# Down-projection of a routed expert layer: wide products on TensorE, the halves summed on VectorE, row weights picked on ScalarE

## What is computed

```
xn  = layernorm(x)
out = x + attn(xn) + ffn(xn)
attn: k = xn @ W_z.T + b_z ; gates by softplus ; cumulative sum over the 256 channels,
      running log-sum-exp over the 1024 steps, one mean and deviation over everything,
      exp, + xn, layernorm with ln_w, ln_b
ffn:  router_logits = xn @ w_gate.T ; softmax ; top 2 of 8 experts, weights made to sum to 1
      for e in 8: h = silu(xn @ w1[e].T) * (xn @ w3[e].T)        # 704 wide
                  out += h @ w2[e].T * expert_weight
```

## Time and profile before

| | us |
|---|---|
| median of the runs shown (356.61 to 356.78) | 356.72 |
| the profiled execution: its own time | 357.79 |
| the profiled execution: its span, first to last instruction | 356.1 |

### The profile page before, as it was taken

How to read it: one execution, slowest core, us unless ns; L and a number is a source line. 1 busy time by engine, 2 the same in 40 slices (tenths; PEclk the granted TensorE clock), 3 DMA queues, 4 the chain that set the end, 5 groups by cost and what they waited for, 6 DMA issues and landing times.

```text
span 356.1 us, 6682 instructions
## 1 busy us (share of the span) xinstructions
PE 325.8 (91%) x1964; PEld 273.9 (77%) x1964; DVE 260.8 (73%) x466; ACT 219.9 (62%) x328; POOL 206.4 (58%) x137
## 2 busy tenths in 40 slices
PE   8998999799999999999898999999999999979830
PEld 8883464588878898997787899889898988969730
DVE  5488787989996899889899842584589668763300
ACT  2547997455879974999854269934853485323400
POOL 4500023159968674989899728563885475945331
PEclk9999969989999999999999999999999999999985
DMA  7924912005444542354354434542463534354621
GB/s 263 426 120 137 293 52 59 15 11 150 122 82 115 142 101 32 80 129 129 44 144 109 102 38 115 142 101 33 84 181 89 75 45 76 47 76 49 98 38 15
DMA packets 19086, 37.00 MB, mean 104 GB/s; under 512 B 2272, under 2 KB 13536, under 8 KB 19008
## 3 DMA queue, kind: packets, MB, share of 16 engines
q0 software_dynamic: 9168, 11.97, 21.5%
q1 hardware_dynamic: 8496, 22.56, 20.4%
q10 hardware_dynamic: 1376, 1.85, 1.4%
HBM read 27.45 MB, written 11.03 MB: 108 GB/s over the span
## 4 chain that ended last, share of the span: by engine, by line
PE 54%; DVE 23%; ACT 8%; issue 8%; DMA 2%; ACTq 1%; POOL 1%; POOLq 0%; DVEq 0%
PE PS L1296 23%; PE PS L1314 11%; PE PS L1190 6%; PE PS L1326 5%; DVE wrow L1067 3%; DVE tmp L961 3%; PE PS L1176 2%; DMA out<-work,sidx 2%; DVE hT L956 2%; DVE U L985 2%; DVE A L998 1%; PE PS L1220 1%; DVE xrow L1054 1%; DVE xrow L1059 1%; PE PS L1265 1%
## 5 line engine op out<-in xcount | busy, mean ns | idle before, releaser
L1296 PE MATMUL PS<-wbuf,xT 128*128 128x512 f32 (+1 forms) x648 | 149.6, 384 | 4.9 <-issue 3.7
L1296 PEld LDWEIGHTS PS<-wbuf,xT 128*128 128x128 f32 x648 | 118.3, 190 | 29.4 <-issue 9.3
L424 POOL TENSOR_TENSOR wbuf<-raw,wbuf x28 | 81.4, 2924 | 23.1 <-ACT wbuf L604 21.4
L406 POOL DMA_INDIRECT out<-work,sidx x35 | 62.7, 1792 | 53.2 <-ACT work L621 20.1
L1314 PE MATMUL PS<-wbuf,hT 128*128 128x256 f32 x648 | 86.8, 288 | 0.0
L1314 PEld LDWEIGHTS PS<-wbuf,hT 128*128 128x128 f32 x648 | 79.3, 189 | 1.9 <-issue 1.9
L390 POOL DMA_INDIRECT work<-xn_dram,gidx x39 | 50.4, 1292 | 51.8 <-DVE gidx L892 36.1
L595 ACT ACTIVATE tmp<-PS 128x512 f32<-128x512 f32 x72 | 32.0, 460 | 41.6 <-PE PS L1296 41.3
L961 DVE TENSOR_TENSOR tmp<-tmp,PS 128x512 f32<-128x512 f32 x72 | 35.0, 516 | 29.4 <-ACT tmp L595 28.6
L956 DVE TENSOR_TENSOR hT<-PS,hT 128x768 fp32r<-128x768 f32 x36 | 34.2, 949 | 29.3 <-ACT hT L590 24.2
L621 ACT ACTIVATE work<-PS,wrow 128x256 f32<-128x256 f32 x35 | 16.4, 470 | 38.0 <-PE PS L1314 38.0
(11 more groups left out here) (185 smaller groups left out, 350.7 us busy)
## 6 DMA issues: line engine op xcount, KB each, us to landing
raw<-w_main SPq DMA_DIRECT2D x24, 544.0 KB
raw<-w_main SPq DMA_DIRECT2D x8, 416.0 KB
xn_dram<-xrow SPq DMA_DIRECT2D x4, 516.0 KB, 7.2
out<-xrow POOLq DMA_DIRECT2D x4, 512.0 KB, 6.1
xrow<-x SPq DMA_DIRECT2D x4, 256.0 KB, 4.8
xrow<-x ACTq DMA_DIRECT2D x4, 256.0 KB, 5.4
small_sb<-small ACTq DMA_DIRECT2D x1, 768.0 KB, 7.9
work<-xn_dram,gidx POOLq DMA_INDIRECT x39
```

Source lines behind the costliest of these rows:

```text
L406: pool.indirect_dma_start(out, bass.IndirectOffsetOnAxis(sidx[:, j:j + 1], 0), ysb[:, j % DEEP, :], None, compute_op=ALU.add).then_inc(s_s ...
L424: pool.tensor_tensor(lo, raw[:, ds(part, WP)], hi.bitcast(fp32), ALU.subtract).then_inc(s_w, 1)
L1296: ins = pe.matmul(PS[:, at:at + cols], xT[:, slot, xpart, q * P:(q + 1) * P], wbuf[:, w, wpart, q * 2 * F + at:q * 2 * F + at + cols], sta ...
```

## The change

Four things change together.

- `down(j)`: the six pieces of the high part of h are each multiplied once by both parts of the weights, side by side (512 columns into a whole PSUM bank, `y_both`), where there were two products of 256 columns. The low part of h is then multiplied by the high part of the weights, into the first half. The result is the sum of the two halves.
- `y_copy(j)` on ScalarE takes only the first half. A new `y_add(j)` on VectorE adds the second half times the row weight; the scatter-add now waits for that (`s_y`), and `y_add` for the copy (`s_ya`). `down(j)` waits for `y_add(j - 1)`.
- The row weight is picked by ScalarE (`row_weight`), ahead of any table load, and no longer by VectorE (`slot_weight`). So that one multiply-add does it, the first extra column of `xrow` becomes the difference of the two routing weights, which is one small VectorE instruction more in the routing part.
- The last tile's y is summed in `last_add`, on VectorE.

```diff
-        y_ps = PS[:, 6 * 512:6 * 512 + D]
+        y_ps = [PS[:, 6 * 512 + n * D:6 * 512 + (n + 1) * D] for n in range(2)]
+        y_both = PS[:, 6 * 512:7 * 512].rearrange("p (n d) -> p n d", n=2)
...
+            def row_weight(j):
+
+                k = j % DEEP
+                act.wait_ge(s_gt[k], 16 * (j // DEEP + 1))
+                act.activation(wrow[:, j:j + 1], xg[:, k, D:D + 1], ACT.Identity, scale=first_pick[:, j:j + 1],
+                               bias=xg[:, k, D + 1:D + 2]).then_inc(s_ws, 1)
...
-                act.activation(ysb[:, j % DEEP, :], y_ps, ACT.Copy, scale=wrow[:, j:j + 1]).then_inc(s_y, 1)
+                act.activation(ysb[:, j % DEEP, :], y_ps[0], ACT.Copy, scale=wrow[:, j:j + 1]).then_inc(s_ya, 1)
...
                     x_hi(j + 1, u % 2)
+                    row_weight(j + 1)
                 if table:
                     act.preload_act_table_set(table)
...
-            dve.tensor_tensor(xrow[:, :, D + 1], w12[:, 1, :], xrow[:, :, D], ALU.mult).then_inc(s_rw, 1)
+            step(dve.tensor_tensor(xrow[:, :, D + 1], w12[:, 1, :], xrow[:, :, D], ALU.mult))
+            dve.tensor_tensor(xrow[:, :, D], xrow[:, :, D], xrow[:, :, D + 1], ALU.subtract).then_inc(s_rw, 1)
...
+            def y_add(j):
+
+                dve.wait_ge(s_ya, j + 1)
+                dve.scalar_tensor_tensor(ysb[:, j % DEEP, :], y_ps[1], wrow[:, j:j + 1], ysb[:, j % DEEP, :],
+                                         ALU.mult, ALU.add).then_inc(s_y, 1)
...
                     x_lo(j + 1, u % 2)
-                    slot_weight(j + 1)
                 if hooks:
                     between(j)
+                y_add(j - 1)
                 h_lo(j)
...
+                    for c in range(HC):
+                        pe.matmul(y_both, hT[:, 0, c * P:(c + 1) * P], wbuf[:, w, :, W13 + c * D:W13 + (c + 1) * D],
+                                  start=(c == 0), stop=False)
+                    hold(pe, s_hlo, j + 1)
+                    for c in range(HC):
+                        ins = pe.matmul(y_ps[0], hT[:, 1, c * P:(c + 1) * P],
+                                        wbuf[:, w, 0, W13 + c * D:W13 + (c + 1) * D],
+                                        start=False, stop=(c == HC - 1))
```

More of the change, by code:

```diff
@@ L259, in build_program @@
         s_dn = sem("down_done")
-        s_y = sem("y_copied")
+        s_ya = sem("y_high_copied")
+        s_y = sem("y_summed")
         s_st = sem("rows_added")
@@ L583, in _ @@
             x_hi(1, 1, xT1_ps)
+            act.wait_ge(s_idx, 1)
+            row_weight(0)
+            row_weight(1)
             h_part(3)
@@ L724, in last_copy @@
                 hold(act, s_dn, used)
-                act.activation(hst[:, 0:D], y_ps, ACT.Copy, scale=wrow[:, NCOL:NCOL + 1]).then_inc(s_y, 1)
+                act.activation(hst[:, 0:D], y_ps[0], ACT.Copy, scale=wrow[:, NCOL:NCOL + 1]).then_inc(s_ya, 1)
             tail(act, tile, last_copy)
@@ L1061, in last_norm @@
                 ins.then_inc(s_p2, 1)
[L1063 to L1068, removed]
             softplus(0)
@@ L1076, in _ @@
             x_lo(0, 0, xT0_ps)
-            slot_weight(0)
             softplus(2)
@@ L1080, in _ @@
             x_lo(1, 1, xT1_ps)
-            slot_weight(1)
             dve.wait_ge(s_u0b, 2)
@@ L1166, in _, with last_add @@
                     tile(i, u, True)
-            tail(dve, tile)
+            def last_add(used):
+                hold(dve, s_ya, used)
+                dve.scalar_tensor_tensor(hst[:, 0:D], y_ps[1], wrow[:, NCOL:NCOL + 1], hst[:, 0:D],
+                                         ALU.mult, ALU.add).then_inc(s_y, 1)
+            tail(dve, tile, last_add)
         @block.tensor
```

## The result

The changed kernel takes 359.42 us (median; 358.22 to 360.75) where the kernel before takes 356.96 (355.92 to 358.39) beside it: a ratio of 1.0068, 95% interval 1.0053 to 1.0082, or +2.4 us (+1.9 to +2.9). The profiled execution took 358.49 us with a span of 356.7; before they were 357.79 and 356.1. The difference of these two is smaller than that of the medians because tile 0 began 1.2 us earlier in the execution after (TensorE's granted clock was 0.979 of full speed there over the span and 0.969 in the one before; the difference lies in the start: 0.97 against 0.94 up to 60 us, 1.00 against 0.91 from 60 to 80 us, and 1.00 in both from 80 to 340 us). So I compare traces from the end of tile 1's gate on.

What follows compares the result with a forecast made beforehand. Bound by TensorE, VectorE or ScalarE depending on the tile, then by GpSimd's queue from tile 26 on. Terms -0.25 + 1.9 + 0.8 + 0 + 0.45 = +2.9 us on 356.72 gave 359.6 us, range 357.0 to 362.0.

Steps and rivals of the forecast that it cites:

- Down-projection: TensorE's products: time goes with columns, so merging saves 0.02 us a tile, -0.25 us over about 12 tiles.
- L1067 leaving VectorE: VectorE: the next two-input instruction takes over the wait for GpSimd's split, or other engines pace the tile; 0 us.
- `row_weight` on ScalarE: One-column ACTIVATE of 0.20 us, counting in tiles 10, 11, 19 and 20, which ScalarE paces; +0.8 us.
- `y_add` on VectorE: 0.38 us each in tiles 2, 3, 15, 16 and 13 or 14, without waiting at the port; +1.9 us.
- Tile 11: A 3.76 us wait ahead of `h_lo` goes, but ScalarE and the tile 12 scan take the gain back; 0.
- y's owner: Scatter-add of tile 25 waits for `y_add`, ready 0.45 us behind ScalarE's copy; +0.45 us, bound 2.2.
- the case of 361.4 us: At tile 25 VectorE is still in `row_stats`, so y is ready at 272.4: +2.2 us.
- The rest of the queue rigid: Behind tile 25's scatter-add, about 85 us of GpSimd issues, landings and splits shift unchanged to the end.
- the order at the port: Rival: VectorE's scans get ahead of GpSimd's L424, each giving back up to 2.9 us; 353.8 us, chance 0.10.
- TensorE by instructions: Rival: a product costs the same at any width, saving 8.5 us over 12 tiles; 351.3 us, chance 0.02.
- no change: Rival: VectorE's additions fit in gaps, or tile 12's scan wins and ScalarE's 0.20 is hidden; 356.7 to 357.4, chance 0.12.
- slower by more: Rival: `y_add` waits for GpSimd's split because of its SBUF scalar, up to 2.5 us each; 363.9 us, chance 0.08.

Runs made afterwards that it cites:

- e2: The kernel before with only the row weight moved from VectorE to ScalarE; 357.43 us, 0.9995 of before.
- e4: The changed kernel without the sum on VectorE, second half of y left out, scatter-adds waiting for ScalarE's copy again; 357.42 us, 1.0006 of before.
- e1: The changed kernel with the row weight back on VectorE; 359.47 us, 1.0055 of before.
- e7: The changed kernel with a second VectorE sum of the same shape ahead of each `y_add`, into an unread buffer; 361.36 us, 1.0117 of before.
- e3: The changed kernel with the sum moved ahead of `row_stats` in tiles 20 to 27; 360.51 us, 1.0094 of before.
- e5: The changed kernel with the sum left out for the rows of tiles 17 on; 359.97 us, 1.007 of before.
- e8: The changed kernel with `y_add` cut to one column, all waits kept; 359.16 us, 1.0063 of before.
- e11: The changed kernel with the 18 narrow products and no sum for rows of tiles 0 to 16; 358.55 us, 1.0056 of before.
- e12: The changed kernel without any sum, the scatter-add of tile 8 also made to wait for `h_lo` of tile 9; 356.69 us, 1.0001 of before.
- e6: The changed kernel with the sum left out for the rows of tiles 0 to 16; 357.5 us, 1.0022 of before.

## Why the prediction was right, point by point

The forecast of +2.9 us was met with +2.4, inside the range and of the sign. Its terms fared less evenly, and that they added up so well is in part luck.

*Down-projection, -0.25.* Right as far as it can be read: about -0.23 in TensorE's starts between e2 and e4, and 2.35 us a group against 2.40. The time goes with columns. Six wide products are a group of 1.65 us. The Trainium skill's TensorE: Matmul & The Clock Gate, section Back-to-back issue gap, gives 131 ns for 512 columns, 0.8 us for six by my estimate; the trace disagrees and decides.

*L1067 leaving VectorE, 0.* In tiles with two-input instructions behind it the wait passed on as forecast (`less_n`, 4.05 us). The step still failed: I forgot its own length, 0.20 us and 0.13 from its begin to the next where nothing waits. Against before, e2 is 0.07 to 0.14 us shorter in each of tiles 2, 3 and 4 and 0.2 in 9 and 10; tile 13 is 0.89 shorter, and 14 gives 0.41 of that back.

*`row_weight` on ScalarE, +0.8.* The instruction is 0.39 us long and moves the next by 0.27, where I took 0.20. In the four places that I named e2 is longer than before by 0.18, 0.14, 0.26 and 0.27 us (the times of tiles 11, 12, 20 and 21), 0.85 in all, so that the term is right; but tiles 6, 7 and 8 pay 0.26, 0.19 and 0.26 too, which I had missed. With what the term above gives back, the balance from tile 1 to 28 is zero, and e1 and e2 measured about that. Their sum in the forecast was +0.8.

*`y_add` on VectorE, +1.9.* The size agrees with the trace of the kernel after, 0.98 + 0.94 us over e4 in tiles 1 to 10 where I had five times 0.38, and e7 nearly doubles it. The places are right in part: I gave tiles 2, 3, 13 or 14, 15 and 16 one each (their times are those of tiles 3, 4, 14 or 15, 16 and 17). The first two and that of tile 15 are there, 0.41 to 0.48 us each over e4, but 0.94 us arise in tiles 8 and 9, which I had called TensorE's alone. VectorE's rows in tile 9 of the kernel after show a chain with no gap, hook, sum, `h_lo`, and three more to the next gate:

```profile
139.52 2.34 DVE L988 TENSOR_TENSOR_SCAN xnT_M<-U,u 128x1024 f32<-128x1024 f32 x1
141.78 0.45 DVE L975 SCALAR_TENSOR_TENSOR work<-PS,wrow,work 128x256 f32<-128x256 f32 x1
142.15 0.94 DVE L970 TENSOR_TENSOR hT<-PS,hT 128x768 fp32r<-128x768 f32 x1
```

The others vanish among waits for splits. That it doesn't wait at the port was right (486 ns at most), with a scalar in SBUF beside one SBUF tensor: here the trace agrees with the Trainium skill's SBUF — State Buffer, section Who interferes with whom, by which at most one SBUF input does not contend.

*Tile 11, 0.* Its mechanism exists and is larger than my bounds. One and the same program up to tile 17 took 62.31 us over tiles 10 to 18 in the profiled execution of the kernel after, 62.29 in that of e3 and 65.41 in that of e5 (362.25 us, its longest). e8 shows +0.97 against e4 with little length. It is the term that I would not again take as a number.

*y's owner, +0.45.* The case that I had as the bound came: the first L1059 (now L1079) got through and the second waited, because GpSimd took the port between two instructions of VectorE (485 ns, then 2754), and y was ready 2.2 us late. By the forecast's own working that is the case of 361.4 us, not of 359.6. Nothing of it reached the end of the profiled execution, so the next step failed as well, and the two errors met.

*The rest of the queue rigid.* It isn't. In e11 and e4, which agree within 0.1 us at tile 25, the scatter-adds stand as follows:

```profile
272.96 1.58 POOL L408 DMA_INDIRECT out<-work,sidx  x1 [3.17 <-DVE work L975]
...
301.74 1.64 POOL L408 DMA_INDIRECT out<-work,sidx  x1 [4.03 <-issue]
...
342.25 1.55 POOL L408 DMA_INDIRECT out<-work,sidx  x1 [2.48 <-DMA out<-work,sidx]
```

```profile
270.84 1.58 POOL L408 DMA_INDIRECT out<-work,sidx  x1 [1.01 <-ACT work L633]
...
289.13 5.05 POOL L426 TENSOR_TENSOR wbuf<-raw,wbuf  x2 [1.40 <-ACT wbuf L616]
...
300.72 1.63 POOL L408 DMA_INDIRECT out<-work,sidx  x1 [3.87 <-issue]
...
342.40 1.55 POOL L408 DMA_INDIRECT out<-work,sidx  x1 [2.46 <-DMA out<-work,sidx]
```

2.12 us at tile 25 are 1.02 at tile 28 and none at 34. The queue has slack of its own, such as the 1.40 us in which GpSimd's split at 289.13 waits for ScalarE.

So the sum came out near for a reason in part. That the sum on VectorE carries the cost is shown (e4 against e1 and the kernel after). That its length is what costs is shown in the traces of tiles 1 to 10 (+1.9), but not for the medians, since one column costs nearly as much. The row weight with L1067's leaving (+0.8) and the queue's +0.45 should have been 0, and two things that I set to zero are not: the order at the port, whose size changes from execution to execution, and whatever makes e11 slow. Two things stay open. By length, e8 should cost 0.8 us and costs 2.2 (1.4 to 3.0); its trace has the missing part at tile 13, but e12, which turned an order in tile 10 on purpose, lost nothing. And the late sums cost nothing on top of the early ones (e5 against after), 0.1 to 1.5 us alone in e6, and 1.1 to 2.9 in e11; no trace here shows the place.

The rivals: TensorE by instructions fell with the 2.35 us against 2.40, "no change" with an interval that starts at +1.9 us, and a door for `y_add`, the case of "slower by more", with the 486 ns. The order at the port turned in several traces and made single tiles shorter as well as longer (tile 13 took 8.01 us in e1), but no kernel was faster by it. The forecast put L926, L968, L985 and L991 just behind the split; in the trace of before it is L1067 that stands there, and they came into that place only when it left.

## What to carry to other kernels

An engine whose time goes with columns gains little from fewer instructions: six products less a tile gave about 0.2 us in all, and one VectorE instruction a tile, which they need, cost about ten times that together with its waits. When an instruction is added to an engine's queue, look for stretches without a gap in its own rows, also where the chain of waits names another engine; 0.94 us of this cost lay there. And where two engines contend for a port, a small edit changed single tiles by 1.2 to 6 us, down as well as up: test such an edit by its time over many executions, since a single trace shows one outcome.

## What the hardware showed

- One column can wait as long as a thousand: a VectorE instruction of 128x1 was 5.64 us long beside a pair of GpSimd's splits (0.15 us alone), and a scan of 128x1024 took 7.56 us instead of 3.44 beside the same pair.
- Who starts first in the trace does not settle who gets the port. The scan of tile 12 began 0.27 us ahead of the split in e8 and waited for it to its end (5.54 us); in the kernel after it began 0.49 us ahead and took 5.75.
- GpSimd's gather is often slower beside a VectorE instruction that reads two SBUF tensors: 1.00 us in e4 and 2.96 in e8 for the same one, which began 0.13 us behind a scan. In all traces here, behind 75 us, no gather that met no such instruction took more than 1.1 us; beside a `TENSOR_TENSOR` they took up to 2.0, beside a `TENSOR_TENSOR_SCAN` up to 2.96, though some stayed at 1.0 there too.
- ScalarE's one-column ACTIVATE with scale and bias from SBUF took 0.38 to 0.40 us; the one without took 0.20.
